# Rotary sums on GpSimd in four pieces instead of two, the queries' pieces first, with a wait of their own for the queries' transposes

## What is computed

```python
q = (x @ Wq.T).reshape(b, t, NH, DH)      # x: normalised tokens, t = 113, NH = 16 heads, DH = 16
k = (x @ Wk.T).reshape(b, t, NH, DH)
v = (x @ Wv.T).reshape(b, t, NH, DH)
q = _apply_rope(q, cos, sin)              # o0 = x0*c - x1*s, o1 = x0*s + x1*c on pairs of elements
k = _apply_rope(k, cos, sin)
att = softmax(einsum('bhqd,bhkd->bhqk', q, k) * DH ** -0.5)
out = einsum('bhqk,bhkd->bhqd', att, v)   # back to (b, t, c), then out @ Wo.T and the residual
```

## Time and profile before

| | us |
|---|---|
| median of 3 runs | 997.22 |
| lowest, highest | 996.27, 998.07 |
| the profiled execution's own time | 997.48 |
| its span | 995.8 |
| busy: PE, PEld | 927.5, 787.5 |
| busy: DVE, ACT, POOL | 712.2, 502.6, 530.8 |

### The profile page before, as it was taken

One profiled execution on the slowest core, in us unless ns is written; L12 is line 12 of the kernel. 1 busy time (PEld: TensorE's weight loads), 2 busy tenths in 40 slices (PEclk: granted clock), 3 DMA queues, 4 the chain that ended last, 5 costly groups with the idle time before them and its releaser, 6 DMA issues. The chain is left out here.

```text
span 995.8 us, 22647 instructions
## 1 busy us (share of the span) xinstructions
PE 927.5 (93%) x8222; PEld 787.5 (79%) x8222; DVE 712.2 (72%) x1047; ACT 502.6 (50%) x817; POOL 530.8 (53%) x430
## 2 busy tenths in 40 slices
PE   4989999999997767799999999999999989999997
PEld 3778888888885455588888888888888649999997
DVE  1357767666674499899999999999998854444442
ACT  1155555555553244466766676667665252333331
POOL 2254222222222076789999999999998352100010
PEclk9899999999999677899999999999999999999999
DMA  8301111111110042132233223322335995667660
GB/s 295 121 27 43 42 41 41 41 40 39 40 39 30 25 96 63 47 96 81 77 83 95 78 68 91 95 73 71 95 85 212 363 415 204 213 225 241 218 186 17
DMA packets 97907, 110.89 MB, mean 111 GB/s; under 512 B 12180, under 2 KB 89012, under 8 KB 91716
## 3 DMA queue, kind: packets, MB, share of 16 engines
q1 hardware_dynamic: 95908, 105.46, 34.1%
q0 software_dynamic: 1376, 3.70, 1.0%
q10 hardware_dynamic: 576, 1.11, 0.3%
HBM read 72.04 MB, written 38.21 MB: 111 GB/s over the span
## 5 line engine op out<-in xcount | busy, mean ns | idle before, releaser
L1223 PE MATMUL slots_p_sum<-slots_x,slots_disp 128*128 128x256 f32 (+1 forms) x928 | 206.9, 380 | 2.2 <-DVE xacc L932 2.2
L1223 PEld LDWEIGHTS slots_p_sum<-slots_x,slots_disp 128*128 128x128 f32 (+1 forms) x928 | 173.4, 190 | 26.9 <-issue 4.2
L1028 POOL TENSOR_TENSOR slots_comb<-slots_comb,slots_cmax 128x1024 f32<-128x1024 f32 (+1 forms) x58 | 111.7, 1944 | 11.3 <-DVE slots_cmax L907 10.3
L1039 POOL TENSOR_TENSOR slots_comb<-slots_comb,slots_csum 128x2048 f32<-128x2048 f32 (+1 forms) x29 | 104.9, 3618 | 19.3 <-DVE slots_csum L861 19.3
L1250 PE MATMUL slots_logits<-phi_hi,slots_xt_hi 128*128 128x512 f32 (+1 forms) x232 | 84.3, 447 | 19.7 <-DVE slots_xt_lo L887 19.7
L1033 POOL TENSOR_TENSOR slots_disp<-slots_disp,slots_dsum 128x2048 f32<-128x2048 f32 (+1 forms) x28 | 102.1, 3645 | 0.0
L1067 POOL DMA_DIRECT2D out<-slots_o x29 | 15.9, 548 | 149.1 <-DVE slots_o L969 149.1
L398 POOL TENSOR_TENSOR attend_stack<-attend_rope_a,attend_rope_b 113x256 f32<-113x256 f32 x64 | 45.3, 729 | 79.7 <-DVE attend_rope_b L353 79.7
L875 DVE TENSOR_TENSOR slots_disp<-slots_logits,slots_dmax 128x512 f32<-128x512 f32 (+1 forms) x116 | 80.1, 691 | 4.2
L1080 ACT ACTIVATE slots_ct<-slots_p_turn 128x512 f32<-128x512 f32 (+1 forms) x116 | 63.9, 577 | 31.2 <-PE slots_p_turn L1211 31.2
L1250 PE MATMUL slots_logits<-phi_lo,slots_xt_hi 128*128 128x512 f32 (+1 forms) x232 | 77.6, 418 | 0.0
(11 more groups left out here) (133 smaller groups left out, 2016.9 us busy)
## 6 DMA issues: line engine op xcount, KB each, us to landing
combine_t<-slots_ct SPq DMA_DIRECT2D x224, 128.0 KB, 2.4
slots_comb<-combine_t SPq DMA_DIRECT2D x14, 1024.0 KB, 5.4
slots_ct<-combine_t SPq DMA_DIRECT2D x14, 1024.0 KB, 5.9
expert_w<-wexp SPq DMA_DIRECT2D x8, 1024.0 KB, 10.0
slots_disp<-wexp SPq DMA_DIRECT2D x8, 1024.0 KB, 14.5
h<-attend_h_out SPq DMA_DIRECT2D x32, 113.0 KB
slots_h_t<-h SPq DMA_DIRECT2D x28, 128.0 KB, 2.3
slots_x<-h SPq DMA_DIRECT2D x28, 128.0 KB, 2.1
```

The lines of the kernel that those rows point to most:

```text
L1028: nc.gpsimd.tensor_tensor(m, m, cmax[0:rows, shalf(i)].unsqueeze(2).broadcast_to([rows, SLOTS // 2, EXPERTS]), ALU.subtract).then_inc(csub ...
L1039: nc.gpsimd.tensor_tensor(m, m, csum[0:rows, 1].unsqueeze(2).broadcast_to([rows, SLOTS, EXPERTS]), ALU.mult).then_inc(comb_ok, 1)
L1223: last = nc.tensor.matmul(p_sum[u % 2][:, i, :], disp[d][0:rows].rearrange("p n s -> p (n s)")[:, 128 * e:128 * e + 128], x[d][0:rows], st ...
```

## The change

GpSimd's sums are cut once more, by queries and keys (`s`): four instructions of 128 elements per partition instead of two of 256, in the order queries even, queries odd, keys even, keys odd. `stack_ok` grows by 4 a batch instead of 2. TensorE waits for the first two pieces ahead of the queries' transposes (`4 * (b + 2) - 2`), and has a new wait for all four ahead of the keys' transposes. VectorE's wait before it overwrites `rope_a` and `rope_b` is adapted to the new count. What is computed and stored is the same.

```diff
--- before.py
+++ after.py
@@ -345,7 +345,7 @@
                 dve.wait_ge(qk_ok, val(b + 3))
-                wait_for(dve, stack_ok, 2 * (b + 2))
+                wait_for(dve, stack_ok, 4 * (b + 2))
@@ -391,12 +391,12 @@
-                by_parity = lambda t: t[:].rearrange("p (a j e) d -> p a j e d", j=GH, e=2)
-                for e in range(2):
-                    dst = stack[par][:].rearrange("p s h r -> p (s h) r").rearrange(
-                        "p (a e j) r -> p a e j r", e=2, j=GH)[:, :, e, :, 0:DH]
-                    nc.gpsimd.tensor_tensor(dst, by_parity(rope_a)[:, :, :, e], by_parity(rope_b)[:, :, :, e],
-                                            ALU.add).then_inc(stack_ok, 1)
+                by_parity = lambda t, s: t[:, HEADS * s:HEADS * (s + 1)].rearrange("p (a j e) d -> p a j e d", j=GH, e=2)
+                for s in range(2):
+                    for e in range(2):
+                        dst = stack[par][:, s].rearrange("p (a e j) r -> p a e j r", e=2, j=GH)[:, :, e, :, 0:DH]
+                        nc.gpsimd.tensor_tensor(dst, by_parity(rope_a, s)[:, :, :, e], by_parity(rope_b, s)[:, :, :, e],
+                                                ALU.add).then_inc(stack_ok, 1)
@@ -525,7 +525,7 @@
             if turns:
-                pe.wait_ge(stack_ok, val(2 * (b + 2)))
+                pe.wait_ge(stack_ok, val(4 * (b + 2) - 2))
                 wait_for(pe, qmax_ok, b)
                 turn_stack(p_q, 1 - par, 0, q_ps_ok)
@@ -541,6 +541,7 @@
             if turns:
+                pe.wait_ge(stack_ok, val(4 * (b + 2)))
                 wait_for(pe, ot_ok, b)
                 turn_stack(p_k, 1 - par, 1, k_ps_ok)
```

## The result

| | before | changed |
|---|---|---|
| median, us | 997.14 (6 runs, 996.27 to 998.17) | 989.35 (6 runs, 988.15 to 991.43) |
| the profiled execution's own time | 997.48 | 990.47 |
| its span | 995.8 | 988.8 |

The ratio is 0.9928, with a 95% interval of 0.9916 to 0.9939: 7.8 us less. The forecast was 990.2 us in a range of 988.6 to 994.0. Run twice more beside the experiments, the same two kernels differed by 7.5 and by 5.9 us (ratios 0.9925 and 0.9937).

A forecast was written before the change was run, and what follows sets the result against it. TensorE was taken to bound the attention loop, standing for GpSimd's sums in steps 4 to 29. 8.1 - 0.9 = 7.2 us saved gives 990.3 us from 997.48, 990.0 from the median; stated 990.2, range 988.6 to 994.0.

The forecast's parts named there:

- The bound and the wait: Attention loop, steps 4 to 29: TensorE's query turns wait for GpSimd's second sum, 7.1 us; half the sums can end it.
- The worth of a step: L525 to shifted scores: removing the wait gives 0.19 or 0.39 us a step, 8.1 us over all.
- 26 x 0.04 us: Steps 4 to 29: each removed wait gives about 0.04 us more than its idle time, added to 7.1 us.
- The size of a piece: GpSimd's sums: a 128-element piece takes 0.46 us by a line through trace rows, bounds 0.36 and 0.729.
- (a): GpSimd's sums: halves cost about 0.60 us, gain only 3.8 us, time 993.5 us; chance 0.11.
- (c): GpSimd's sums: half size costs nearly the same, start loses 4.1 us, loop gains nothing, time 1001.6 us; chance 0.05.
- Early enough: Query turns in the loop: first two pieces ready early by 0.12 us in step 24 and 0.31 in step 23.
- What is late next: Second query turns: VectorE's maximum (L314) comes 0.03 us ahead, costing nothing but capping the gain.
- The keys and the added wait: Keys' turns: sums end 0.3 us later, covered by over a microsecond; TensorE's new wait costs 0.
- rival (d): TensorE's new wait interrupts the stream, up to 0.17 us in some 29 steps, time 995.2 us; chance 0.06.
- The start: Steps 0 to 2, where GpSimd has no idle time: four pieces add 0.29 us a step, 0.9 us lost.
- The sum: Whole kernel: 8.1 us gained less 0.9 lost, 7.2 us saved, time 990.2 us.

The follow-up runs named there:

- e1: Changed kernel with the queries' transposes waiting for all four pieces instead of the first two: 1006.28 us, ratio 1.0107 to before.
- e2: Changed kernel with pieces ordered queries even, keys even, queries odd, keys odd, and the queries' transposes waiting for three: 995.25 us, ratio 0.9990 to before.
- e7: Changed kernel with the low parts of the router's weights (L413) moved later in GpSimd's queue: 989.79 us, ratio 0.9944 to before.
- e4: Changed kernel with VectorE's maximum (L314) taken over 56 of 113 keys only: 988.21 us in its one execution.
- e3: Changed kernel with five waits on stack_ok instead of one ahead of the keys' transposes: 991.9 us, ratio 0.9961 to before.
- e6: Changed kernel with two sums of 256 elements, queries then keys, heads reordered on the host: 989.85 us, ratio 0.9932 to before.
- e9: Changed kernel with two sums (queries, keys), router's low parts moved, and GpSimd beginning them only after VectorE's L342: 986.59 us, ratio 0.9901 to before.

## Why the prediction was right

**The bound and the wait.** Right. The turns waited for the second sum, half of the sums ended the wait, and the gain came in the steps named. (Step 30 had waited too, for 0.14 us, which the list of the earlier trace rows doesn't print; it became 0.09 us shorter.) e1 and e2 show it as a dose: queries ready after two pieces 257.0 us for the middle, after three 262.35, after four 273.98, against 263.67 before.

**The worth of a step.** Its size was a little off. I took 7.1 us of idle time and 26 x 0.04 us on top, 8.1 in all; step 4 to step 31 gave 7.55. From L525 to the shifted scores the even steps of the loop gave 0.36 to 0.39 us and the odd ones 0.17 to 0.24, each only 0.01 to 0.03 more than its standing time (at the edges, step 4 gave 0.18 and step 29 0.44). The term that was mis-sized is the 26 x 0.04 us; some 0.4 us of it came. The forecast's own values for single steps would have done better: 13 x (0.19 + 0.39) = 7.5.

**The size of a piece.** 0.46 us from the line of one, 256 and 512 elements; measured 457 ns, and 1.70 us for four against 1.72. The line through the rows of the trace held, down to 128 elements:

```profile
L398 POOL TENSOR_TENSOR attend_stack<-attend_rope_a,attend_rope_b 113x128 f32<-113x128 f32 x128 | 54.4, 457 | 80.4 <-DVE attend_rope_b L353 80.4
```

Rivals (a) and (c) end here.

**Early enough.** The result was right, the margin not. I had 0.12 us for even steps. In step 20 the sums begin at 218.75, and its first two pieces (a timeline cut off at 219.3) take 0.87 us:

```profile
218.75 0.87 POOL L398 TENSOR_TENSOR attend_stack<-attend_rope_a,attend_rope_b 113x128 f32<-113x128 f32 x2 [2.45 <-DVE attend_rope_b L353]
```

So the queries are ready at about 218.75 + 0.87 + 0.05 = 219.67, and the turns start at 219.71: 0.04 us, and 0.02 to 0.05 in the even steps of the loop. The sums of these steps begin 0.1 us later than before, which nothing in the trace of before showed, and which e1 and e2 made visible as standing time. With pieces 0.03 us dearer, half of the steps would have waited again: that the whole wait went was in part luck. In e7, where no sum begins late, the margin is the 0.12 us of the forecast.

**What is late next.** Nothing: e4 halved the maximum and the steps kept their length. In the changed kernel the second turns of every step from 4 to 29 start 0.05 us behind the maximum's end, which is also the distance of a released wait, so the two come together to within hundredths, as forecast.

**The keys and the added wait.** No standing before the keys' turns. One wait is free, five are not (e3), so rival (d) was wrong by size for one wait. My reason, that a met wait costs 0 to 0.002 us, was too general: it held for one wait here and not for four more.

**The start.** 0.9 us lost by the sum, 0.86 measured, and gone to the hundredth in e6, where GpSimd works no longer than before.

**The sum.** 7.2 us forecast, 6.7 in the two parts that the change touches, 7.0 in the profiled executions, 7.8 between the medians, and 7.5 and 5.9 when the pair was run again. Whole times scatter by more than the forecast missed by, so how close 990.2 came to 989.35 is partly luck; the 6.7 us of the middle are what tests the forecast, with the miss in the term named above.

## What to carry to other kernels

When an engine waits for a result of which it needs only a part at first, ask whether that part alone comes before everything else that the engine must do; take the worth from steps of the same trace that happened not to wait, and look for the margin on the producer's side, since here it was 0.02 to 0.05 us. Cutting an instruction costs its fixed time again, which must be added up where the producer has no idle time (here in three steps); a change of layout that lets the same number of instructions serve in another order avoids it. And before work is moved into an engine's idle time, look at what then runs beside it on the other engines.

## What the runs showed of the hardware that I had not expected

A VectorE tensor_scalar from SBUF to SBUF (L342, 113x256, fp32) is held up by a GpSimd tensor_tensor (128x1024) that began before it: 0.41 us alone, 2.46 and 2.44 us when begun 0.06 and 0.07 us after a GpSimd instruction of 2.36 and 2.37 us, and 0.41 again when GpSimd waits for its end (e7 and e9). The other way round, VectorE first, no run shows. The Trainium skill has this rule (SBUF — State Buffer, Who interferes with whom): VectorE operations in a two-port mode, which tensor_scalar can enter, and GpSimd share one pair of ports, the first to start holds it for its whole instruction, and the other is blocked. The trace agrees with the blocking: L342 ended at 65.94 us, L384 at 65.78. These 0.16 us (0.14 the second time) are less than the 0.41 that L342 takes alone, so part of its time did pass beside the subtraction. The same section says that a tensor_reduce never contends on trn2. The trace agrees, for one that reads PSUM: L314 ran beside GpSimd's sums for 1.0 us in step 20 of the changed kernel, against 0.65 in step 24 before, and kept its time, as its line in the changed kernel shows (duration ns min/median/max):

```profile
L314 DVE TENSOR_REDUCE attend_stack<-attend_p_score x32: 2023/2043/2045, 52.6 to 314.4; 113x16 f32<-113x1808 f32 x32
```

In the changed kernel and in e1 to e4, GpSimd's first sum begins 0.25 instead of 0.16 us after the rotation's end in the even steps of the loop (0.52 in step 4), and not in the kernel before and e6, which have two sums a step. The number of sums isn't the cause, since e7 has the same four in the same loop and begins all of them at 0.16; it differs only in instructions outside the loop. Why was not tried; it is open.
